# Causal mask: from a bf16 matmul into the score banks to an addition on VectorE

## The reference, cut to what matters

```
q, k, v = heads(layernorm(x) Wq), heads(ctx Wk), heads(ctx Wv)   # 16 heads of 16
scores  = rope(q) * 16**-0.5 @ rope(k).T                          # 112 x 112 a head
mask    = (key > query) | (key < query - 128)                     # the second never holds
probs   = softmax(where(mask, lowest, scores))
x       = x + tanh(g_xattn) * ((probs @ v) Wo + bo)
...                                                               # experts: unchanged
```

## Time and profile before

| | us |
|---|---|
| median of 3 runs | 872.85 (867.83 to 877.78) |
| the profiled execution, whole | 870.56 |
| its span in the trace | 868.8 |
| TensorE matmuls busy | 699.3 (80%), 5192 instructions |
| VectorE busy | 514.7 (59%), 1333 |
| ScalarE busy | 389.9 (45%), 1574 |
| GpSimd busy | 333.5 (38%), 346 |

### The profile page before, as it was taken

How to read it: one execution, slowest core, us unless ns; L and a number is a source line. 1 busy time by engine, 2 the same in 40 slices (tenths; PEclk the granted TensorE clock), 3 DMA queues, 4 the chain that set the end, 5 groups by cost and what they waited for, 6 DMA issues and landing times.

```text
span 868.8 us, 17566 instructions
## 1 busy us (share of the span) xinstructions
PE 699.3 (80%) x5192; PEld 544.2 (63%) x5192; DVE 514.7 (59%) x1333; ACT 389.9 (45%) x1574; POOL 333.5 (38%) x346
## 2 busy tenths in 40 slices
PE   6879999898998989898877300008999999999993
PEld 3456666566665665666644200006999999999993
DVE  5354776667676676763894588892544444454442
ACT  1256676766767666676642243301222222222220
POOL 2524344442634434360201002003556655655642
PEclk9979999999999999997787555556999999999997
DMA  5330010202002020100101401001888888898841
GB/s 151 98 123 17 15 56 23 65 24 59 26 1 64 23 64 22 41 2 1 43 2 42 165 0 21 0 0 34 262 261 256 256 266 259 245 279 253 250 101 17
DMA packets 57278, 84.45 MB, mean 97 GB/s; under 512 B 11266, under 2 KB 28032, under 8 KB 57216
## 3 DMA queue, kind: packets, MB, share of 16 engines
q1 hardware_dynamic: 48000, 74.01, 25.9%
q0 software_dynamic: 9216, 9.76, 7.0%
HBM read 71.05 MB, written 12.69 MB: 96 GB/s over the span
## 4 chain that ended last, share of the span: by engine, by line
PE 58%; DVE 21%; ACT 9%; issue 5%; POOL 2%; DMA 2%; DVEq 1%; ACTq 0%; SPq 0%; POOLq 0%
PE pair L786 18%; PE bank L796 9%; PE pair L1324 5%; PE bank L1280 5%; ACT arena L1052 5%; DVE arena L1218 3%; DVE arena L592 3%; PE pair L1333 3%; PE bank L1285 3%; PE bank L1352 3%; DVE arena L641 3%; PE pair L1319 2%; PE bank L1292 2%; PE bank L1304 2%; PE bank L806 2%
## 5 line engine op out<-in xcount | busy, mean ns | idle before, releaser
L1052 ACT ACTIVATE arena<-pair,arena 112x112 f32<-112x112 f32 x512 | 175.1, 362 | 130.6 <-DVE arena L1218 130.5
L786 PE MATMUL pair<-arena,we 128*128 128x140 f32 x1024 | 141.0, 287 | 0.7 <-ACT arena L707 0.6
L786 PEld LDWEIGHTS pair<-arena,we 128*128 128x128 f32 x1024 | 131.2, 193 | 1.9 <-issue 1.9
L750 DVE SCALAR_TENSOR_TENSOR arena<-arena,pair 128x140 f32<-128x140 f32 x160 | 47.6, 298 | 139.9 <-ACT arena L715 139.9
L692 POOL DMA_INDIRECT rows_out<-arena,slot_row x64 | 94.4, 1475 | 93.9 <-DVE arena L739 76.0
L715 ACT ACTIVATE arena<-pair 128x140 f32<-128x140 f32 x160 | 45.9, 287 | 150.0 <-PE pair L786 150.0
L1052 ACT ACTIVATION_READ_ACCUMULATOR arena<-pair,arena 112x1 f32 x512 | 108.4, 212 | 0.0
L1218 DVE TENSOR_REDUCE arena<-pair 112x8 f32<-112x896 f32 x64 | 69.3, 1083 | 49.6 <-PE pair L1324 49.6
L925 POOL TENSOR_TENSOR arena<-arena,tab 128x448 f32<-128x448 f32 x32 | 36.3, 1134 | 148.6 <-DVE we L1132 148.4
L683 POOL DMA_INDIRECT arena<-rows,slot_row x64 | 62.5, 976 | 71.5 <-issue 71.5
L796 PE MATMUL bank<-arena,we 128*128 128x140 f32 x512 | 83.4, 286 | 0.0
(11 more groups left out here) (184 smaller groups left out, 1230.4 us busy)
## 6 DMA issues: line engine op xcount, KB each, us to landing
we<-w_experts_in SPq DMA_DIRECT2D x192, 256.0 KB, 4.3
wa<-w_adapters_in SPq DMA_DIRECT2D x16, 384.0 KB, 5.6
arena<-ctx_in SPq DMA_DIRECT2D x8, 448.0 KB, 4.5
arena<-x_in SPq DMA_DIRECT2D x8, 448.0 KB, 3.9
rows_out<-arena SPq DMA_DIRECT2D x8, 448.0 KB, 3.3
rows<-arena SPq DMA_DIRECT2D x8, 448.0 KB, 3.4
arena<-rows,slot_row POOLq DMA_INDIRECT x64, 4.0
rows_out<-arena,slot_row POOLq DMA_INDIRECT x64
```

The source lines that it names most:

```text
L750: signal(dve, nc.vector.scalar_tensor_tensor(gs[m % 2], th[m % 2], 1.0, banks[m % 4][:, 0:CAP], ALU.add, ALU.mult), s_gs, n + 1)
L786: last = nc.tensor.matmul(banks[m % 4][:, part * CAP:(part + 1) * CAP], w[:, col0:col0 + 128], xet[j % 2][:, c, :], start=(c == 0), stop=( ...
L1052: last = nc.scalar.activation(pr[s % 2][:, j, :], banks[BS[s % 4]][0:T, j * T:(j + 1) * T], ACT.Exp, bias=nmx[s // 2 % 2][:, s % 2, j:j + ...
```

## The change

The two mask matmuls of a pair are gone, and the first score matmul of each region starts the accumulation. VectorE adds the f32 mask (from the table, the same for both units and all heads) to the scores of a pair and writes the sum to a new SBUF buffer `masked`, of which there are two. The maximum and the exps read that buffer and no longer the banks. VectorE waits for its own addition before the maximum (`link`), and before the addition for the exps of the pair that used the buffer last. The arena grows by 1460 words.

```diff
-POOL_LINKS, DVE_LINKS = 22, 20
+POOL_LINKS, DVE_LINKS = 22, 36
...
-    ARENA = 25440
+    ARENA = 26900
...
+    masked = [take(T, [2, HU, T]) for _ in range(2)]
...
-                        last = nc.scalar.activation(pr[s % 2][:, j, :], banks[BS[s % 4]][0:T, j * T:(j + 1) * T],
+                        last = nc.scalar.activation(pr[s % 2][:, j, :], masked[s // 2 % 2][:, s % 2, j, :],
...
                     wait(dve, s_s, GU * g + s + 2)
-                    nc.vector.tensor_reduce(nmx[s // 2 % 2], pairs[s // 2 % 2][0:T, :, 0:HU * T].rearrange(
-                        "p u (h k) -> p u h k", h=HU), X, ALU.max, negate=True).then_inc(s_mx, 1)
+                    wait(dve, s_exp, GU * g + s - 2)
+                    link(nc.vector.tensor_tensor(
+                        masked[s // 2 % 2], pairs[s // 2 % 2][0:T, :, 0:HU * T].rearrange("p u (h k) -> p u h k", h=HU),
+                        tab[0:T, TAB["causal"]].unsqueeze(1).unsqueeze(1).to_broadcast([T, 2, HU, T]), ALU.add))
+                    nc.vector.tensor_reduce(nmx[s // 2 % 2], masked[s // 2 % 2], X, ALU.max,
+                                            negate=True).then_inc(s_mx, 1)
...
                 wait(pe, s_pte[i], GU // 2 * g + s // 2 - 1)
-                nc.tensor.matmul(banks[BS[(s + i) % 4]][0:T, 0:HU * T], identb,
-                                 causalb.unsqueeze(1).to_broadcast([T, HU, T]), start=True, stop=False)
...
-                                            start=False, stop=(t == 1))
+                                            start=True, stop=True)
```

## The result

| | before | changed |
|---|---|---|
| median, us | 870.97 (867.83 to 877.78, 4 runs) | 923.00 (921.37 to 924.13, 4 runs) |
| the profiled execution, whole / span | 870.56 / 868.8 | 921.37 / 919.6 |

The ratio is 1.0609 (95% interval 1.0563 to 1.0654): 52 us slower. 912 was forecast, with 893 to 931 as the range.

A forecast was written before the change was run, and what follows sets the result against it. Bound: a chain along TensorE in some steps, through scores, maximum, exp and probability copy in others. 870.6 plus 42 (33.5 six repeating groups, 6.6 first and last, 2 exps) gave 912.6; 912 was said, range 893 to 931.

The forecast's parts named there:

- Direction and bound: Whole kernel: slower by over 1%, chance 0.91, since the chain of waits leaves TensorE in some steps of a group.
- Rival C: TensorE is the bound after all, additions fit VectorE's idle time, only the masks count: -25 us, 848; chance 0.04.
- rival A: The clock drops a second time in each attention group, up to 1.7 us each: 12 us more, 924; chance 0.25.
- The signs: Profile signs if right: VectorE's busy time up some 70 us, group about 56.8, exps' idle over 180, TensorE near 79%.
- The addition: 64 additions of 112x896 on VectorE: 1.09 us each, 1.12 with the wait, between scores and maximum.
- The maximum's source: VectorE's maximum reading SBUF: no gain by the rows; 0.065 us less each by the Trainium skill, some 2.6 in all.
- The exps' source: ScalarE's exps reading SBUF: +3.7 us at most by the rows, 2 taken; +6.9 by the Trainium skill.
- The walk: One repeating group, from a pair's first score matmul to the next pair's: 5.6 us longer, 33.5 for six groups.
- First and last group: First and last attention group, by count: five additions less six masks, 3.3 us each, 6.6 together.

The follow-up runs named there:

- run 2: The kernel before with the mask matmuls left out and nothing in their place: 857.6 us, ratio 0.9803.
- run 12: The kernel before without its maximum (exps with bias zero), mask matmuls kept: 823.1 us, ratio 0.9436.
- Run 11: The changed kernel without its maximum (exps with bias zero), so the addition stands in the maximum's place: 870.6 us, ratio 0.9998.
- run 3: The kernel before with the exps reading a constant SBUF buffer instead of the banks: 875.9 us, ratio 1.0067.
- Run 4: The changed kernel with the exps reading the unmasked scores in the banks again: 926.6 us, ratio 1.0646.
- Run 8: The kernel before with an SBUF-to-SBUF addition of the same size once a pair on VectorE, behind maximum and probability copy, result unused: 921.5 us, ratio 1.0613.
- run 6: The changed kernel with addition and maximum taken unit by unit (448 elements each): 913.1 us, ratio 1.0503.
- run 9: The changed kernel with short bf16 filler matmuls of 64 columns in TensorE's gaps: 933.5 us, ratio 1.0709.
- run 7: The kernel before with the maximum alone taken unit by unit, mask matmuls kept: 851.6 us, ratio 0.9807.
- 10: The changed kernel with addition and maximum unit by unit, plus short bf16 filler matmuls in TensorE's gaps: 920.6 us, ratio 1.0538.
- run 5: The changed kernel with eight f32 filler matmuls of 64 columns before TensorE's wait for the spread sums: 948.1 us, ratio 1.0914.

## Why the prediction was right, point by point

- **Direction and bound.** Right, and shown: TensorE at 93% wasn't the only limit. Taking its masks away alone gives 12 us at the median (run 2), taking VectorE's maximum away 49 (run 12). Rival C would have needed 848, with the addition in place; even without it only one execution of four came so low. The 923 lies 11 above the 912 and 1 below rival A's 924, but it did not come about by A's mechanism, as the points below show.
- **The signs.** Held: the addition, VectorE's busy time (69 us more for 70), the unchanged maximum, line 1367 (then 1364) waiting for ScalarE in all four of its steps. A group came out at 57.95 to 58.3 us for 56.8, the first at 60.3. Missed: the exps' idle time behind VectorE, 160.8 us of 173.7 for over 180; TensorE's busy share, 82% of a group (76% of the span) for 79%. The clock over the six groups, 0.90, stood on the edge of rival A's sign.
- **The addition**, 1.09 and 1.12 with its wait: measured 1.086; the maximum starts 0.04 us behind it (289.38 + 1.09, then 290.51). Right. Run 11 shows that it has no further cost: in the maximum's place it costs what the maximum did, but for the 7 us that are left open there.
- **The maximum's source.** No gain, 1.088 for 1.083. The 0.065 us less by the figures of the Trainium skill (VectorE: DVE Perf Modes, section on the TRN2 errata) didn't show.
- **The exps' source: the term that was mis-sized.** I had taken 2 us, half of the rows' 3.7, in case the accumulator reads covered it. Alone it costs 6 (run 3), and the exps are spaced 0.043 us wider. By the figures of the same section of the Trainium skill an exp costs 0.043 us more; the trace agrees, and the estimate of 6.9 us in all that the prediction made from it was nearer than the copies of other shapes in the earlier trace rows. In the table of intervals 0.17 us a unit, in five intervals, would be 0.9 of the 1.2 us by which the group is longer than forecast. Run 4, which took it back, didn't get it back; why is open, beyond its lower clock.
- **The walk.** The five additions and the missing masks fell where it had put them; no interval is off by more than 0.4 us, with step 0 counted as in the table (by its first two matmuls 0 to 2 would be 1.2 over and 12 to 0 0.7 under). What it rested on was put too narrowly: I spoke of the latency from scores to exps. Run 8 shows that an addition which no exp waits for also costs 52 us, though part of that is its own longer records, as VectorE's next maximum stands behind it in the queue; and run 6 that a shorter way to the first exps, with 1.3 us more of VectorE's work a group, gives back 10 of 52 us. The idle time of VectorE, 16 us a group by busy time, was no free room: in the group from 290.2 to 341.4 us it ended 6.6 us in waits for ScalarE's line 1065, 4.1 at the turn of the loop, 3.5 for scores and 1.7 for POOL, and most of the rest behind its own instructions.
- **First and last group.** By count 6.6 us; measured 5.6 + 4.8 = 10.4. The count left out the loops that come up, which the walk had for the repeating groups. That is argued from the intervals: in the first group 4 to 6, 6 to 8, 10 to 12 and 12 to 14 grew by 1.0 to 1.4 us each.
- **Rival A.** The second low stretch came (0.91 in a group, 309.84 to 316.83 the new one), but is worth 0.45 us there and nothing at step 8, some 3 us over six groups by my estimate (0.45 from one pair of steps, against run 9); only the first repeating group, at 0.86, shows more (60.3 us for 57.95 to 58.3). By that my price of 12 us was too high, for the reason that I had given against it. It is an estimate and not shown: the fillers never held the clock up through a whole group, and between executions of one kernel the clock goes with up to 12 us (run 2) and 10 us (run 6).
- **Where the sum came out low.** By the profiled executions it was 912.6 against 921.4, 9 us. The six repeating groups have 43.8 for the 35 that I had priced (33.5 and their share of the exps), 9 more. By estimate some 4 are the exps (0.9 a group less the 1.5 priced), some 3 the low clock of steps 12 to 14, some 2 the first of these groups; no run separates them. The first and last group have 3.5 more, and the work behind took 3.5 less, which is luck: it lies within what that work varies by. The other 2 us to 923 are the median of the four runs over the profiled one.

## What to carry to other kernels

Before work is moved to an engine that looks 40% idle, read what ends its idle times. Waits for the others in a loop are no room, and in an in-order queue work behind one critical instruction is ahead of the next. Price a move by walking from one occurrence of the loop's head to the next, and take the bound engine's busy time at its full clock. Where the loop goes by a pair of small operations in series, halving their grain (run 7) can be worth more than moving them.

## What the runs showed of the hardware

- Exps of 112 elements with a bias and an accumulator follow one another at 0.333 us from the banks (kernel before, run 4) and at 0.376 from SBUF (changed kernel, runs 3 and 11), mean of 384 each; the accumulator read is shorter from SBUF (0.188 for 0.212), which doesn't make up for it.
- A two-operand f32 addition of 896 elements on VectorE takes 1.086 us on average with one operand in the banks (1.03 to 1.10 over 64, changed kernel). With both in SBUF it takes 1.08 at the median and up to 1.98 (run 8); all 21 of 64 above 1.2 us overlapped an addition of GpSimd, and two others did so too and took 1.08.
- Where its loop comes round VectorE stands 4.0 to 4.9 us with no releaser that the profile shows (kernel before, runs 2, 3, 6 to 8, 10 and 11, and once in run 4). In the kernel before it ends ahead of the scores; in runs 6 and 8 the two groups with it are 2 to 4 us longer than their neighbours.
- A 64-column f32 matmul with its weight load took 0.22 us in a row of eight (1.78, run 5), a bf16 one 0.06 (1.22 for 20, run 9).
- Two score matmuls of 32 rows started beside a six-row matmul (267.06 and 267.04 us, changed kernel) once no mask matmul of 112 rows stood between them.
